# Who widens the counts: two of ten tiles move from GpSimd to VectorE, one from ScalarE to VectorE

## The chip, the cores and the metric

The kernel runs on one core of a Trainium2 chip. The time is the device time of one execution in microseconds (us). The core has a matrix engine (TensorE, PE), three engines for elementwise work (VectorE is DVE, ScalarE is ACT, GpSimd is POOL) and DMA queues. Every engine runs its own instructions strictly in program order and waits for the others on semaphores.

## The reference, cut to what matters

The model is a chain of four graph layers on 1250 nodes with 512 features and 20000 edges. The first two layers contain a mean over the neighbours of a node:

```
agg = jax.ops.segment_sum(x[src], dst, num_segments=n)          # layer 0
mean_agg = agg / jnp.maximum(cnt, 1.0)[:, None]
...
agg = jax.ops.segment_sum(msg, edge_index[1], num_segments=N)   # layer 1, msg = xn[edge_index[0]]
agg = agg / jnp.maximum(deg, 1.0)[:, None]
```

The kernel does each of these sums as a matrix product of the features with a matrix of edge counts.

## The kernel before, in words

The edge counts are built once, in the first 165 us, as an int16 matrix `cntT` of ten tiles: 125 source nodes on the partitions, 1250 destination nodes along the row. [...]

An aggregation (`aggregate` on TensorE) loops over four blocks `k` of 128 features, and in each over the ten tiles `j`. For one tile it issues six matmuls: two halves of the fp16-split features (`h_pair`) times three column pieces (512, 512, 226) of the widened tile. All ten tiles add up in one PSUM tensor `psW[k % 2]`. A group of three tiny matmuls closes the block and signals `agg_full`. VectorE then multiplies the block by the reciprocal degree into `aggT`, in one instruction in layer 0 and in a pair in layer 1, and signals `agg_taken` (and `agg_read`). Block k may start when block k-2 has been taken.

The widened tiles live in a ring of four buffers (`QUAD = 4`). Tile number n, counted over all blocks and both layers, may be written when TensorE has used tile n-4 (`cT_used` at n-3 or more). ScalarE writes tiles 0, 1, 2, 3, 4, 6, 7, 8 of each block (`BY_ACT`, through its helper `copy`, so the profile shows line 526). GpSimd writes tiles 5 and 9 (`BY_POOL`, line 464). TensorE waits for each tile by the count of whoever makes it (`widened`). A further branch for counts above 2048 (`big`) isn't taken.

Program order of VectorE around the two aggregations:

- Layer 0: `ln_stats(0)` ends with ten copies and splits of the normalised features (lines 897 and 900); the last split lets TensorE start. Then four instructions over 1250 columns prepare the reciprocal degree (lines 975 to 978). Then, per block, `counts_of_block` waits for `agg_full` and line 981 takes the block.
- Layer 1: behind the barrier `phase_end(dve, 3)` four pairs of additions correct `hT` (lines 1083 and 1084). Then, per block, the wait for `agg_full` and the pair of lines 1094 and 1096. Ahead of that wait, in blocks 1 and 2, stands `score_weights` (lines 1077 to 1080), ten instructions that prepare layer 2.

ScalarE and GpSimd have nothing but the widening to do during the blocks. Behind the four blocks TensorE goes on with the dense product of the layer.

Of the kernel before, what the change touches and what calls it, by code (L numbers as in the profile page):

```python
# [22 lines left out]
TILES, ROWS = 10, 125  # L23
KD = D // 128
# [22 lines left out]
QUAD = 4  # L47
# [27 lines left out]
def gnn_program(nc, a, out, layers=4):  # L75
    ctx = ExitStack()
    with ctx:
# [11 lines left out]
        cntT = sb("cntT", [128, TILES, N], I16)  # L89
# [63 lines left out]
        def region(off, shape, dt=F32):  # L153
# [47 lines left out]
        cntT_16 = [[region(o, [N], F16) for o in base] for base in (  # L201
            [G + 14750 + 625 * i for i in range(5)], [G + 14750, G + 15375, G + 5000, G + 5625, G + 6250])]
# [69 lines left out]

            return ps[:, 0:2 * PB * VA].rearrange("p (h b d) -> p h b d", h=2, b=PB)

        BY_ACT = (0, 1, 2, 3, 4, 6, 7, 8)
        BY_POOL = (5, 9)

        def widened(l, k, j):

            own, signal = (BY_POOL, "cP_wide") if j in BY_POOL else (BY_ACT, "cT_wide")  # L280
            return signal, len(own) * (l * KD + k) + own.index(j) + 1

        def acc_view(ps):
# [6 lines left out]
            edge_cols group_bounds bounds_turned bounds_set consts_set hot0_made hot1_made hot2_made hot3_made  # L290
            hot0_free hot1_free hot2_free hot3_free tile_counted counts_f32 mask_made bars_set counts_turning
            counts_turn_read deg_split deg_turned deg_row_out deg_wide ln_ready h_made h_turned hT_made
            x_plus_h h1_made h_split cT_wide cT_used cP_wide lo_wide lo_made lo_used agg_full agg_taken agg_read w_turned
            w_turn_read y_full y_out y_stats y_scaled y_started z_turned x_updated  qk_full qk_out v_full v_out
            proj_turned proj_out sq_made diag_full diag_out uk_full uk_max kmax_all kbias_set kf_exp
            kf_made uq_full uq_max qf_exp  qf_turned qfT_out kv_full kv_out at_full at_out at_turned
# [6 lines left out]
        S = {n: sem(n) for n in names}  # L303
# [18 lines left out]
        def after(eng, signal, count):  # L322

            if not isinstance(count, int) or count > 0:
                eng.wait_ge(S[signal], count)
# [128 lines left out]
        @block.gpsimd  # L454
        def _(pool):
            done = Order(pool, S["pool_done"])

            def widen(l):

                for k in range(KD):  # L460
                    for j in BY_POOL:
                        n = TILES * (l * KD + k) + j
                        pool.wait_ge(S["cT_used"], n - QUAD + 1)
                        pool.tensor_copy(cntT_16[l][n % QUAD][0:ROWS, :], cntT[0:ROWS, j, :]).then_inc(S["cP_wide"], 1)

            many = dict(allow_small_or_imprecise_dtypes=True, channel_multiplier=0)
            done(pool.memset(ident[:, :], 1.0))
            pool.affine_select(out=ident[:, :], in_=ident[:, :], compare_op=ALU.is_equal, fill=0.0, base=0,
                               pattern=[[-1, 128]], channel_multiplier=1).then_inc(S["ident_set"], 1)
            pool.memset(bar_c[:, :], BARRED).then_inc(S["bars_set"], 1)  # L470
            pool.iota(tile_lo, pattern=[[ROWS, TILES]], base=0, **many)
            pool.iota(up_row, pattern=[[1, GROUPS]], base=1, **many)
            done(pool.iota(down_row, pattern=[[-1, GROUPS]], base=GROUPS, **many))
            done(pool.memset(zero_bf[:, :], 0.0))
            pool.iota(iota_h[:, :], pattern=[[1, N]], base=0, **many).then_inc(S["consts_set"], 1)
            pool.memset(keps_c[:, :], KEPS)
            done(pool.memset(half_c[:, :], 0.0))
            for r in range(2):
                pool.memset(half_c[DH * r:DH * r + DH, r:r + 1], 0.5)
            done(pool.memset(sel[:, :, :], 0.0))  # L480
            for r in range(3):
                done(pool.affine_select(out=sel[:, :, :], in_=sel[:, :, :], compare_op=ALU.not_equal, fill=1.0, base=-r * TILES,
                                        pattern=[[-1, TILES], [0, 128]], channel_multiplier=1))
            pool.wait_ge(S["ident_set"], 1)
            pool.tensor_copy(ident_bf[:, :], ident[:, :]).then_inc(S["sel_set"], 1)
            pool.memset(hint_c[:, :], HINT)
            done(pool.memset(fold[:, :], 0.0))
            for r in range(2):
                done(pool.affine_select(out=fold[:, :], in_=fold[:, :], compare_op=ALU.not_equal, fill=1.0, base=-r * DH,
                                        pattern=[[-1, DH]], channel_multiplier=1))  # L490
            pool.memset(barred_c[:, :], -BARRED)
            done(pool.memset(ident_neg[:, :], 0.0))
            pool.affine_select(out=ident_neg[:, :], in_=ident_neg[:, :], compare_op=ALU.not_equal, fill=-1.0, base=0,
                               pattern=[[-1, 128]], channel_multiplier=1)
            done(pool.affine_select(out=sel_w[:, :], in_=ident_bf[:, :], compare_op=ALU.is_ge, fill=1.0, base=ROWS - 1,
                                    pattern=[[0, 128]], channel_multiplier=-1))

            phase_end(pool, 1)

            for t in range(TILES):  # L500
                pool.wait_ge(S["h_made"], t + 1)
                pool.tensor_tensor(x_nm[0:ROWS, t, :], x_nm[0:ROWS, t, :], h32[t % RING][0:ROWS, :], ALU.add).then_inc(S["x_plus_h"], 1)
            widen(0)
            phase_end(pool, 2)
            for i in range(2):
                half = slice(H // 2 * i, H // 2 * i + H // 2)
                pool.wait_ge(S["uk_max"], H // 2 * (i + 1))
                pool.partition_all_reduce(kmaxa[:, half], kmax[:, half], 128, RMAX).then_inc(S["kmax_all"], 1)
            phase_end(pool, 3)
            widen(1)  # L510
            phase_end(pool, 4)
            pool.wait_ge(S["hT_made"], 3 * TILES)
            pool.memset(v_gat[0:ROWS, :, :, DH], 1.0).then_inc(S["ones_set"], 1)
            pool.wait_ge(S["cols_out"], 1)
            for h in range(1, H):
                shift_of(pool, done, h)
            phase_end(pool, 5)
            pool.wait_ge(S["w_maxed"], 1)
            pool.partition_all_reduce(w_all[:, :], w_most[:, :], 128, RMAX).then_inc(S["w_spread"], 1)
            phase_end(pool, 6)  # L520
# [3 lines left out]
        def _(act):  # L524
# [77 lines left out]
            def widen(l, big):  # L602

                for k in range(KD):
                    for j in BY_ACT:
                        n = TILES * (l * KD + k) + j
# [196 lines left out]
        def _(dve):  # L803
# [82 lines left out]
            def ln_stats(l):  # L886
# [8 lines left out]
                for t in range(TILES):  # L895
                    dve.wait_ge(S["h_turned"], TILES * l + t + 1)
                    dve.tensor_copy((hT if l < 3 else hT3)[:, :, t * ROWS:(t + 1) * ROWS], psS[t % 2][:, 0:KD * ROWS].rearrange("p (k c) -> p k c", k=KD)).then_inc(S["hT_made"], 1)
                    if l < 2:
                        dve.wait_ge(S["h1_made"], TILES * l + t + 1)
                        stt(h_pair[1][0:ROWS, t, :], h32[t % RING][0:ROWS, :], HS, h_pair[0][0:ROWS, t, :], ALU.mult, ALU.subtract).then_inc(S["h_split"], 1)  # L900

            def counts_of_block(l, k, big):

                with dve.If(big > 0):
                    for j in range(TILES):
                        dve.wait_ge(S["lo_wide"], TILES * (l * KD + k) + j + 1)
                        tt(cntT_16[l][QUAD][0:ROWS, :], cntT[0:ROWS, j, :], cntT_16[l][QUAD][0:ROWS, :], ALU.subtract).then_inc(S["lo_made"], 1)
                dve.wait_ge(S["agg_full"], l * KD + k + 1)
# [63 lines left out]

            big = has_big_count(dve)
            ln_stats(0)
            done(ts(rdeg_b, pos_b, 1.0, None, ALU.max))
            done(dve.reciprocal(rdeg_b, rdeg_b))
            done(ts(rdeg_b, rdeg_b, 1.0 / HS, None, ALU.mult))
            done(ts(pos_b, pos_b, 1.0, None, ALU.min))
            for k in range(KD):
                counts_of_block(0, k, big)  # L980
                tt(aggT[:, k, :], psW[k % 2][:, 0:N], rdeg_b, ALU.mult).then_inc(S["agg_taken"], 1)
            dve.wait_ge(S["vec_in"], 16 * 10)
# [3 lines left out]
            if layers >= 2:  # L986
# [86 lines left out]
                def score_weights(r):  # L1073
# [5 lines left out]
                    done(tt(prod, wb_row, half, ALU.mult))  # L1079
                    return dve.tensor_reduce(c16[:, own], prod, AX, ALU.add)  # L1080

                for f in range(KD):
                    tt(hT[:, f, 0:NPERF], hT[:, f, 0:NPERF], oT[:, f, :], ALU.add)
                    done(ts(hT[:, f, NPERF:N], hT[:, f, NPERF:N], oT[:, f, NPERF - 1:NPERF], None, ALU.add))
                for k in range(KD):
                    if k == 1:
                        dve.wait_ge(S["w_gat_in"], 16 * KD)
                        dve.wait_ge(S["gat_w_in"], 48)
                        done(score_weights(0))
                        done(tt(c16[:, 0:H], c16[:, 0:H], ab_row, ALU.add))  # L1090
                    if k == 2:
                        score_weights(1).then_inc(S["wa_made"], 1)
                    counts_of_block(1, k, big)
                    stt(aggT[:, k, :], psW[k % 2][:, 0:N], scl1[:, k:k + 1], rdeg_b, ALU.mult, ALU.mult).then_inc(S["agg_taken"], 1)
                    dve.wait_ge(S["agg_taken"], KD + k + 1)
                    stt(aggT[:, k, :], pos_b, shf1[:, k:k + 1], aggT[:, k, :], ALU.mult, ALU.add).then_inc(S["agg_read"], 1)
# [656 lines left out]
```

## Time and profile before

| | us |
|---|---|
| median of 3 runs | 1310.76 |
| lowest, highest | 1310.09, 1312.12 |
| the profiled execution, whole | 1311.84 |
| its span, first to last instruction | 1310.1 |

In the profile, a group line names line, engine, operation and tiles, then the count, the busy time and the mean of one in ns, and the idle time before it with what ended it. A timeline row is start, length, engine, line, operation, count of merged instructions and, in brackets, the idle time ahead of it and who ended it. A windows row gives the busy time of each engine in a stretch with the number of instructions, then the clock that TensorE was granted (1.00 is 2.4 GHz, 0.50 is 1.2 GHz) and the DMA share. A waits row is the waiting line, what it waited for, the sum in us, how many times, and the longest.

### The profile page before, as it was taken

Reading aid. Unit: us, or ns where it says so; the run is one execution under the profiler, and the core shown is the slowest. Engines: PE = TensorE matmul, PEld = TensorE weight load, DVE = VectorE, ACT = ScalarE, POOL = GpSimd, SP = SyncE. Lnnn points to the kernel's source line nnn. Section 1 sums busy time; section 2 is a strip of 40 time slices with the busy share of each in tenths; the row PEclk is TensorE's granted clock in tenths of the full one; section 3 lists DMA queues with packets and bytes.
Section 4 is the critical chain, followed back from the end, with each engine's and each line's share of the span. In section 5 each row is a group of like instructions: output and inputs, shape, how many; then the busy total and the mean of one; then the engine's idle time right before and its main releaser. Section 6 shows DMA issues by size and latency. Waiting matters only on the chain.

```text
span 1310.1 us, 16906 instructions
## 1 busy us (share of the span) xinstructions
PE 1178.8 (90%) x5857; PEld 736.3 (56%) x5857; DVE 924.0 (71%) x1663; ACT 708.2 (54%) x885; POOL 65.2 (5%) x115
## 2 busy tenths in 40 slices
PE   4999959997998986979999999859988999999996
PEld 3666635554785544435444544434545777777775
DVE  6999873105455697778998896673116888888885
ACT  1232368202556667148778777531115777777774
POOL 3000042000001100000000000000000000000000
PEclk8999959997899996979999999979997999999999
DMA  4000000003003000201111100020011111110102
GB/s 148 5 1 1 1 1 2 1 1 129 1 1 89 2 1 1 81 23 42 42 42 42 42 23 3 1 96 1 1 24 25 25 26 25 26 25 1 26 1 79
DMA packets 24769, 36.15 MB, mean 28 GB/s; under 512 B 11874, under 2 KB 13204, under 8 KB 24694
## 3 DMA queue, kind: packets, MB, share of 16 engines
q1 hardware_dynamic: 24694, 35.14, 9.0%
q8 instruction: 49, 0.80, 0.3%
q14 instruction: 26, 0.21, 0.1%
HBM read 26.03 MB, written 2.70 MB: 22 GB/s over the span
## 4 chain that ended last, share of the span: by engine, by line
PE 56%; DVE 11%; ACT 5%; issue 3%; DMA 0%; SPq 0%; ACTq 0%; DVEq 0%; POOLq 0%
PE wide L58 15%; PE wide L1613 12%; PE wide L1243 7%; PE small L1697 5%; PE wide L1601 3%; PE wide L1603 3%; PE small L1655 2%; ACT arena L797 2%; PE small L1243 2%; DVE arena L1126 2%; PE wide L1402 1%; PE small L1710 1%; DVE arena L1150 1%; DVE bn L812 1%; DVE bns L915 1%
## 5 line engine op out<-in xcount | busy, mean ns | idle before, releaser
L58 PE MATMUL wide<-arena 125*125 (+7 forms) x2028 | 487.2, 389 | 33.3 <-DVE arena L873 12.6
L58 PEld LDWEIGHTS wide<-arena 125*125 (+4 forms) x2028 | 270.6, 141 | 226.7 <-issue 144.1
L1613 PE MATMUL wide<-arena 125*65 125x512 f32 (+1 forms) x480 | 181.5, 514 | 0.0
L1243 PE MATMUL small<-ident,arena 125*128 125x125 f32 (+5 forms) x438 | 85.8, 347 | 62.1 <-ACT arena L593 32.0
L1150 DVE TENSOR_TENSOR arena<-wide,arena 125x1250 f32<-125x1250 f32 x80 | 116.7, 1459 | 35.2 <-PE wide L1603 35.2
L725 ACT ACTIVATE arena<-arena,b 125x1250 f32<-125x1250 f32 x80 | 106.7, 1336 | 58.4 <-PE wide L1613 54.0
L782 ACT ACTIVATE arena<-wide 125x1000 f16<-125x1000 f32 x80 | 80.8, 1010 | 80.8 <-PE wide L1243 80.8
L1243 PE MATMUL wide<-ident,arena 125*125 125x125 f32 (+2 forms) x874 | 116.8, 282 | 6.5 <-ACT arena L797 3.5
L797 ACT ACTIVATE arena<-arena,neg_max,unit 125x1250 f32<-125x1250 f32 x80 | 114.3, 1429 | 10.5 <-DVE neg_max L1231 10.5
L1613 PEld LDWEIGHTS wide<-arena 125*65 125x65 f32 x480 | 63.1, 138 | 101.0 <-issue 94.5
L1204 DVE SCALAR_TENSOR_TENSOR arena<-wide,arena 125x1000 f16<-125x1000 f32 x80 | 95.9, 1198 | 33.8 <-ACT arena L782 33.8
L1126 DVE CUSTOM_DVE_ANT_0 arena<-arena,cnt 125x1250 bf16<-125x1250 f32 x80 | 116.1, 1451 | 1.5 <-DVE b_max L1126 1.5
L1697 PE MATMUL small<-arena 125*128 125x250 f16 x800 | 112.7, 271 | 1.4 <-DVE arena L1206 1.4
L1243 PEld LDWEIGHTS small<-ident,arena 125*128 125x128 f32 (+5 forms) x438 | 69.2, 218 | 78.9 <-issue 37.0
L1243 PEld LDWEIGHTS wide<-ident,arena 125*125 125x125 f32 (+2 forms) x874 | 104.6, 188 | 14.8 <-ACT arena L797 8.0
L872 DVE TENSOR_SCALAR arena<-arena 125x1250 f16 x196 | 106.1, 541 | 7.2 <-issue 5.5
L754 ACT ACTIVATE arena<-arena,b 125x1250 f32<-125x1250 f32 x80 | 105.8, 1324 | 5.8 <-DVE arena L1150 5.8
L526 ACT ACTIVATE arena<-wide 65x512 f32<-65x512 f32 (+4 forms) x50 | 29.7, 641 | 133.5 <-PE wide L1305 110.3
L1697 PEld LDWEIGHTS small<-arena 125*128 125x128 f16 x800 | 72.1, 98 | 27.8 <-issue 20.2
L526 ACT ACTIVATE arena<-cntT 125x1250 f16<-125x1250 int16 x64 | 74.5, 1233 | 14.3 <-PE wide L58 14.1
L1601 PE MATMUL wide<-arena,sel_w 128*125 128x512 bf16 (+1 forms) x240 | 58.2, 351 | 12.5 <-DVE arena L1150 9.1
L1228 DVE CUSTOM_DVE_ANT_0 arena<-wide,cnt 125x1250 f32<-125x1250 f32 x40 | 58.0, 1451 | 10.8 <-PE wide L58 10.8
(241 smaller groups left out, 1221.0 us busy)
## 6 DMA issues: line engine op xcount, KB each, us to landing
arena<-rows_kept SPq DMA_DIRECT2D x16, 625.0 KB, 5.6
arena<-arena SPq DMA_DIRECT2D x40, 156.2 KB, 2.8
arena<-in_L_gnn_W SPq DMA_DIRECT2D x3, 1024.0 KB, 7.6
x_nm<-in_x SPq DMA_DIRECT2D x2, 1250.0 KB
out<-x_nm SPq DMA_DIRECT2D x1, 2187.5 KB
arena<-in_L_gnn_W_l SPq DMA_DIRECT2D x1, 1024.0 KB, 5.8
arena<-in_L_gnn_W_r SPq DMA_DIRECT2D x1, 1024.0 KB, 8.1
arena<-in_L_gnn_Wk SPq DMA_DIRECT2D x1, 1024.0 KB, 5.5
```

Source lines behind the costliest of these rows:

```text
L58: mm = pe.matmul(ps[0:rows, lo:hi], lhsT, rhs[:, lo:hi], start=start, stop=stop, skip_group_check=True)
L526: return act.activation(dst, src, ACT.Copy, **k)
L725: act.activation(ring[n % RINGS][0:ROWS, :], t_bc[h % 2][0:ROWS, :], ACT.Relu, scale=0.8, bias=b08[0:ROWS, h, t:t + 1]).then_inc(S["relu2_ ...
L754: act.activation(row, row, ACT.Exp, bias=b02[0:ROWS, h, t:t + 1]).then_inc(S["exp2_made"], 1)
L797: act.activation(row, row, ACT.Exp, bias=neg_max[0:ROWS, n % TILES:n % TILES + 1], scale=unit[0:ROWS, 0:1], accum_out=den3[0:ROWS, n:n + 1 ...
L872: ts(hot_src[0:ROWS, n % 2, g, :], iota_h[0:ROWS, :], e_col[0:ROWS, 1, k, g:g + 1], None, ALU.is_equal)
L1126: dve.tensor_tensor_reduce(junk[0:ROWS, :], b_bc[h % 2][0:ROWS, :], mask[0:ROWS, i, :], 1.0, 2 * NEG, ALU.subtract, ALU.max, b_max[0:ROWS, ...
L1150: tt(row, psW[0][0:ROWS, 0:N], row, ALU.add).then_inc(S["z2_made"], 1)
L1243: return pe.transpose(dst, src, ident[0:k, 0:k])
L1601: pe.matmul(psW[0][0:ROWS, lo:hi], sel_w[:, 0:ROWS], ln_hi[:, t, lo:hi], start=True, stop=False)
L1613: m = pe.matmul(psW[1][0:VA, lo:hi], v_gat[0:ROWS, t, h, :], ring[n % RINGS][0:ROWS, lo:hi], start=(t == 0), stop=(t == TILES - 1))
L1697: m = pe.matmul(small[:, 0:2 * ROWS], v_pair[0:ROWS, j, h, :, :].rearrange("p c d -> p (c d)"), turned[pair % 2][0:ROWS, j, 2 * part:2 * p ...
```

## The change

Tiles 3, 6 and 9 of each block are widened by VectorE, the other seven by ScalarE, none by GpSimd. The rule of the ring and the order in which TensorE uses the tiles stay. VectorE's three casts of a block are put into its program as one group, with the waits on `cT_used` between them: block 0 of layer 0 behind `ln_stats(0)` and ahead of line 975; block 0 of layer 1 ahead of lines 1083 and 1084; every later block at the head of its turn of the loop, so ahead of `score_weights` in layer 1 and behind the instructions that take the previous block.

```diff
-        BY_ACT = (0, 1, 2, 3, 4, 6, 7, 8)
-        BY_POOL = (5, 9)
+        BY_ACT = (0, 1, 2, 4, 5, 7, 8)
+        BY_DVE = (3, 6, 9)
...
-            own, signal = (BY_POOL, "cP_wide") if j in BY_POOL else (BY_ACT, "cT_wide")
+            own, signal = (BY_DVE, "cV_wide") if j in BY_DVE else (BY_ACT, "cT_wide")
...
@@ GpSimd: the helper and both calls, widen(0) and widen(1), go
-                        pool.wait_ge(S["cT_used"], n - QUAD + 1)
-                        pool.tensor_copy(cntT_16[l][n % QUAD][0:ROWS, :], cntT[0:ROWS, j, :]).then_inc(S["cP_wide"], 1)
...
@@ VectorE
+            def widen(l, k):
+                for j in BY_DVE:
+                    n = TILES * (l * KD + k) + j
+                    after(dve, "cT_used", n - QUAD + 1)
+                    dve.tensor_copy(cntT_16[l][n % QUAD][0:ROWS, :], cntT[0:ROWS, j, :]).then_inc(S["cV_wide"], 1)
...
             ln_stats(0)
+            widen(0, 0)
             done(ts(rdeg_b, pos_b, 1.0, None, ALU.max))
             done(dve.reciprocal(rdeg_b, rdeg_b))
             done(ts(rdeg_b, rdeg_b, 1.0 / HS, None, ALU.mult))
             done(ts(pos_b, pos_b, 1.0, None, ALU.min))
             for k in range(KD):
+                if k >= 1:
+                    widen(0, k)
                 counts_of_block(0, k, big)
...
+                widen(1, 0)
                 for f in range(KD):
                     tt(hT[:, f, 0:NPERF], hT[:, f, 0:NPERF], oT[:, f, :], ALU.add)
                     done(ts(hT[:, f, NPERF:N], hT[:, f, NPERF:N], oT[:, f, NPERF - 1:NPERF], None, ALU.add))
                 for k in range(KD):
+                    if k >= 1:
+                        widen(1, k)
                     if k == 1:
                         dve.wait_ge(S["w_gat_in"], 16 * KD)
```

## Rows read from the trace of the kernel before

**Rows 1.** The page: busy time of the engines; then the chain that ended last.

```profile
PE 1178.8 (90%) x5857; PEld 736.3 (56%) x5857; DVE 924.0 (71%) x1663; ACT 708.2 (54%) x885; POOL 65.2 (5%) x115
...
PE 56%; DVE 11%; ACT 5%; issue 3%; DMA 0%; SPq 0%; ACTq 0%; DVEq 0%; POOLq 0%
```

**Rows 2.** Windows over one inner block of layer 0 and of layer 1.

```profile
206.84:217.60 10.76, 10.76 (x63) 5.77 (x60) 1.46 (x1) 9.15 (x9) 2.46 (x2) 1.00 0.01 2
418.53:429.30 10.77, 10.77 (x63) 5.77 (x61) 10.35 (x11) 9.16 (x9) 3.12 (x2) 1.00 0.01 2
```

**Rows 3.** Waits: PE and ACT in 193.5 to 240, PE in 405.5 to 452.

```profile
PE wide L58 <- DVE arena L900: 2.4, 1, 2.4
...
ACT arena L526 <- PE wide L58: 8.6, 8, 2.2
...
PE wide L58 <- ACT arena L526: 3.3, 1, 3.3
```

**Rows 4.** Timeline of layer 0 around its first block.

```profile
193.46 0.80 DVE L975 TENSOR_SCALAR arena<-arena 128x1250 f32<-128x1250 f32 x1
...
193.59 13.16 PE L58 MATMUL wide<-arena 125*128 125x512 f16 x60 [2.44 <-DVE arena L900]
...
194.29 7.97 DVE L976 RECIPROCAL arena<-arena 128x1250 f32<-128x1250 f32 x1
...
202.55 1.63 POOL L464 CAST arena<-cntT 125x1250 f16<-125x1250 int16 x1 [3.32 <-PE wide L58]
203.13 1.72 DVE L978 TENSOR_SCALAR arena<-arena 128x1250 f32<-128x1250 f32 x1
...
206.84 10.84 PE L58 MATMUL wide<-arena 125*128 125x512 f16 x60
206.95 1.46 DVE L981 TENSOR_TENSOR arena<-wide,arena 128x1250 f32<-128x1250 f32 x1 [2.10 <-PE wide L1340]
```

**Rows 5.** Timeline of layer 1 across its first three blocks.

```profile
404.48 0.43 DVE L1083 TENSOR_TENSOR arena<-arena 128x256 f32<-128x256 f32 x1 [0.35 <-ACTq L319]
...
408.14 0.73 DVE L1084 TENSOR_SCALAR arena<-arena 128x994 f32<-128x994 f32 x1
...
414.25 1.22 POOL L464 CAST arena<-cntT 125x1250 f16<-125x1250 int16 x1 [3.19 <-PE wide L58]
...
418.64 1.52 DVE L1094 SCALAR_TENSOR_TENSOR arena<-wide,scl,arena 128x1250 f32<-128x1250 f32 x1 [9.76 <-PE wide L1340]
420.19 1.52 DVE L1096 SCALAR_TENSOR_TENSOR arena<-arena,shf 128x1250 f32<-128x1250 f32 x1
...
421.63 1.71 DVE L1077 TENSOR_TENSOR arena<-arena 128x512 f32<-128x512 f32 x1
...
431.01 1.52 DVE L1094 SCALAR_TENSOR_TENSOR arena<-wide,scl,arena 128x1250 f32<-128x1250 f32 x1 [0.25 <-DVE c L1090]
...
434.29 0.68 DVE L1077 TENSOR_TENSOR arena<-arena 128x512 f32<-128x512 f32 x1
...
441.57 1.51 DVE L1094 SCALAR_TENSOR_TENSOR arena<-wide,scl,arena 128x1250 f32<-128x1250 f32 x1
```

**Rows 6.** Groups of VectorE by line and shape: nearest operations to the new cast.

```profile
L872 DVE TENSOR_SCALAR arena<-arena 125x1250 f16 x196 | 106.1, 541 | 7.2 <-issue 5.5 <-PE wide L58 1.6
...
L931 DVE TENSOR_TENSOR arena<-arena 125x1250 bf16<-125x1250 f32 x10 | 14.5, 1453 | 6.9 <-ACT arena L620 6.7
```

**Rows 7.** Windows around idle stretches of PE, for the granted clock.

```profile
402.63:405.97 3.34, 0.00 (x1) 0.03 (x2) 2.55 (x12) 2.69 (x7) 0.00 (x0) 1.00 0.07 9
...
406.60:410.00 3.40, 3.40 (x12) 1.43 (x10) 2.21 (x5) 3.40 (x4) 0.16 (x1) 0.50 1.06 338
...
826.50:828.60 2.10, 0.30 (x3) 0.06 (x2) 2.10 (x3) 1.41 (x2) 0.00 (x0) 1.00 0.00 0
...
878.50:880.90 2.40, 0.00 (x1) 0.00 (x0) 2.10 (x10) 1.26 (x2) 0.00 (x0) 1.00 0.00 0
...
881.10:884.30 3.20, 3.20 (x4) 1.17 (x4) 1.97 (x3) 0.00 (x0) 0.00 (x0) 0.50 0.00 0
```

More of the change, by code:

```diff
@@ L292, in gnn_program @@
             counts_turn_read deg_split deg_turned deg_row_out deg_wide ln_ready h_made h_turned hT_made
-            x_plus_h h1_made h_split cT_wide cT_used cP_wide lo_wide lo_made lo_used agg_full agg_taken agg_read w_turned
+            x_plus_h h1_made h_split cT_wide cT_used cV_wide lo_wide lo_made lo_used agg_full agg_taken agg_read w_turned
             w_turn_read y_full y_out y_stats y_scaled y_started z_turned x_updated  qk_full qk_out v_full v_out
@@ L456, in _ @@
             done = Order(pool, S["pool_done"])
[L458 to L462, printed above, removed]
-                        pool.wait_ge(S["cT_used"], n - QUAD + 1)
-                        pool.tensor_copy(cntT_16[l][n % QUAD][0:ROWS, :], cntT[0:ROWS, j, :]).then_inc(S["cP_wide"], 1)
             many = dict(allow_small_or_imprecise_dtypes=True, channel_multiplier=0)
@@ L502, in _ @@
                 pool.tensor_tensor(x_nm[0:ROWS, t, :], x_nm[0:ROWS, t, :], h32[t % RING][0:ROWS, :], ALU.add).then_inc(S["x_plus_h"], 1)
-            widen(0)
             phase_end(pool, 2)
@@ L509, in _ @@
             phase_end(pool, 3)
-            widen(1)
             phase_end(pool, 4)
```

## Prediction

> **What bounds the kernel now.** I read the page first: TensorE is busy 90% of the span, and on the chain that ended last it holds 56% against 11% for VectorE and 5% for ScalarE [rows 1]. That is an average over six stages, and the change touches two of them, so I took the windows over single blocks next. An inner block has TensorE busy from end to end at clock 1.00 in both layers (10.76 of 10.76 us, 10.77 of 10.77 us) [rows 2]. The waits say the same from the other side: through the four blocks of layer 0 TensorE waited once, at their start, 2.4 us for VectorE's last split, and through those of layer 1 once, 3.3 us for the first widened tile. ScalarE, on the contrary, waited eight times for TensorE to free a buffer [rows 3]. So the supply of widened tiles is never late today. Its makers run ahead until the ring of four is full. A block takes 10.84 us for 60 matmuls, 1.084 us a tile, and 10.92 us from start to start with the closing group (206.84 + 10.92 = 217.76) [rows 4]. No part of the change touches this, so it has nothing to gain there. The question is only whether VectorE delivers tiles 3, 6 and 9 in time. A tile 3 is wanted 3.25 us after its block starts.
>
> VectorE is idle through most of a block of layer 0 (1.46 us busy), but not in layer 1 (10.35 us busy in the second block) [rows 2]. And an in-order engine is late by what stands ahead of an instruction, not by its busy share.
>
> **The cost of one cast.** The trace shows no int16 to fp16 copy on VectorE. Below, the nearest row is a one-input operation on 125x1250 of 2-byte data, 0.541 us; above, the slow rate of an operation of this length, 1.453 us [rows 6]. I take 0.54, the row nearest in size, width of data and number of inputs, and keep 1.45 for the range. Going from one instruction to the next costs VectorE 0.03 us (193.46 + 0.80 to 194.29) [rows 4]. The first matmul starts 0.05 us behind the end of what it waited for (the split ahead of 193.59 ended at 193.54).
>
> A rule to weigh here: the Trainium skill, "VectorE: DVE Perf Modes", section "The perf-mode tier table", gives a copy of 2-byte data in SBUF four elements a cycle and 693 ns for 2048 of them. By its breakdown (some 158 fixed cycles and 1250/4 at 0.96 GHz) the cast would take an estimated 0.49 us, and the sum below would be 0.4 us less. No run here shows whether the conversion from int16 keeps that rate; without it the upper bound applies.
>
> **Layer 0.** Tiles 0 to 2 come from ScalarE as before, tile 3 from VectorE right behind the split, well ahead of need. Then VectorE stands at tile 9, which may be written once tile 5 has been used. GpSimd's cast of tile 9 waited for the same event and began at 202.55 [rows 4]. Behind this wait now stand lines 975 to 978, which began at 193.46 before. From the start of line 975 to that of line 978 is 9.67 us, nearly all of it the 7.97 us reciprocal [rows 4]. Line 978 costs a further 0.80 like line 975; its 1.72 in the trace includes a delay beside a GpSimd cast. So:
>
> 202.55 + 0.54 + 0.03 (tile 9) = 203.12; + 9.67 + 0.84 = 213.63; line 981 takes block 0, + 1.46 + 0.03 = 215.12; tile 3 of block 1, + 0.54 + 0.05 = 215.7.
>
> TensorE wants that tile at 206.84 + 3.25 = 210.1. **Stall 5.6 us** in block 1. In blocks 2 and 3 VectorE has only line 981 ahead of tile 3: 0.11 + 1.49 + 0.54 = 2.1 us after the block's end against some 3.4, hidden, and hidden also with a cast of 1.45. ScalarE's casts are ready sooner in the stall and cost nothing.
>
> **Layer 1, block 0 to 1.** `widen(1, 0)` goes ahead of the corrections of `hT`, and waits for tile 5 of block 0: GpSimd began on the same event at 414.25 [rows 5]. The corrections took 404.48 to 408.87 (408.14 + 0.73), 4.39 us [rows 5]. 414.25 + 0.57 + 4.42 = 419.24. `agg_full` is there by then; the pair of lines 1094 and 1096 takes 3.07 us (418.64 to 421.71), so 422.34; tile 3, + 0.54 + 0.05 = 422.9. It is wanted at 418.53 + 3.25 = 421.8. **Stall 1.1 us.**
>
> **Block 1 to 2.** From now on VectorE's round from one tile 9 to the next tile 3 sets the pace. It starts when tile 5 has been used: 0.15 to notice, 0.57 for tile 9, `score_weights(0)`, the pair 3.10, tile 3 with 0.59. From line 1077 at 421.63 to line 1094 at 431.01 is 9.38 us, of which the first instruction took 1.71 where its twin took 0.68 [rows 5], and a third one was longer by 0.71 beside the next GpSimd cast. Without casts there it is 7.6. Sum 12.0 us. TensorE itself needs, from tile 5 used to tile 3 wanted, four tiles, the closing group and three tiles: 4.34 + 0.15 + 3.25 = 7.74. **Stall 4.3 us.**
>
> **Block 2 to 3.** The same with `score_weights(1)`, 434.29 to 441.57, 7.28 us [rows 5]: 0.15 + 0.57 + 7.28 + 3.10 + 0.59 = 11.7 against 7.74. **Stall 3.9 us.** Behind block 3 everything follows as before, later by the sum.
>
> Here a rule counts on the change's side. The clearest row is line 1077, 1.71 us where its twin took 0.68 [rows 5]. The Trainium skill, "GPSIMD Engine Reference", section "Specifications", has GpSimd's SBUF interfaces shared with VectorE, with contention for instructions with two SBUF inputs, and line 1077 is one; the trace agrees. The sum above already uses undisturbed durations; with the disturbed ones it would be about 2.6 us higher.
>
> **The clock.** After 2.40 us of idleness ending at 880.90 TensorE ran at 0.50 in 881.10 to 884.30, and after 3.34 us ending at 405.97 at 0.50 in 406.60 to 410.00; after the 1.80 us within 826.50 to 828.60 it stayed at 1.00 [rows 7]. The stalls of 5.6, 4.3 and 3.9 us lie with the former, that of 1.1 with the latter. A fall costs half the time spent at 0.50: 3.40 us make 1.7. At the upper end is the first block of layer 0, which began slow and took 13.16 us against 10.84, 2.3 more [rows 4]. I take 2.0 three times, **6.0 us**. The slow tiles come right behind the stall, before tile 5, so VectorE's next round doesn't hide them.
>
> **Sum.** 5.6 + 1.1 + 4.3 + 3.9 = 14.9, and 6.0 for the clock: 20.9 us more. GpSimd's sixteen casts and ScalarE's eight end off the path and give nothing back. The profiled execution took 1311.84 us in all for a span of 1310.1, which makes 1332.7; it was 1.1 above the median of the runs, so the predicted median is 1310.76 + 20.9 = **1331.7**.
>
> **The rivals.**
> - *The stalls come, the clock holds.* It speaks for it that each stall is short against the stage and dense matmuls stand around it; against it, the fall after 2.40 us. 14.9 more: 1325.7.
> - *The cast runs at the slow rate.* Each of the four late rounds holds two casts, so 8 x 0.91 = 7.3 us on top: 20.9 + 7.3 = 28.2, 1339.0. The conversion of the type speaks for it, the 0.541 us row against it.
> - *Not slower: the tile supply paces TensorE.* The six matmuls of a tile have 2500 columns, 1.042 us at 2.4 GHz, and take 1.084. If the gap were waiting for ScalarE's signals, seven casts instead of eight would close part of it: up to 8 x 0.4 = 3.2 us less, 1307.6. It decides only where VectorE's round stays below TensorE's 7.74 us; reckoned, it is 12.0. ScalarE's eight waits for TensorE speak against it [rows 3].
> - *Deeper loss.* Falls of the clock last longer, or catch the 1.1 us stall as well: 3 to 5 us more, 1335 to 1337.
>
> **How the numbers follow.** Forecast 0.66, its own range 1327 to 1336; clock holds 0.12; slow cast 0.09; deeper loss 0.08; not slower 0.05. The range 1324 to 1340 takes in both bounds of the cast and both of the clock. A measurement tells about 0.2% (2.6 us) from no change. Of the last case 0.02 is faster and 0.02 the same, and 0.01 is a small loss; all others are slower: 0.96.
>
> **What would show it.** In the waits, TensorE's matmuls of line 58 wait for VectorE's cast four times, 5.6, 1.1, 4.3 and 3.9 us, each at tile 3 of a block; none in blocks 2 and 3 of layer 0. Line 975 starts near 203 instead of 193.5. The group of the cast shows 24 instructions of 0.54 us. The windows behind the three long stalls show 0.50 for 3 to 5 us. Line 1077 shows no 1.71. The prediction is wrong if TensorE is busy through blocks 1 as before, if the wait falls on another tile or engine, or if the loss is outside the two aggregations.

## The result and the profile after

| | before, us | changed, us |
|---|---|---|
| median | 1311.44 (4 runs) | 1333.07 (4 runs) |
| lowest, highest | 1310.09, 1312.67 | 1330.12, 1333.29 |
| span of the profiled execution | 1310.1 | 1331.5 |

The ratio is 1.016, 95% interval 1.0142 to 1.0178: 21.6 us slower, where 20.9 had been forecast. The title counts the change net; tile by tile, 9 goes from GpSimd to VectorE, 3 and 6 from ScalarE to VectorE, and 5 from GpSimd to ScalarE.

First the waits of the changed kernel, TensorE only, for the stretch from 193.5 to 250 and then for 405 to 480 (waiting line, what it waited for, sum in us, times, longest). Line 897 is VectorE's new cast, which widens one tile from int16 to fp16.

```profile
PE wide L58 <- DVE arena L897: 5.4, 1, 5.4
PE wide L58 <- DVE arena L890: 2.4, 1, 2.4
...
PE wide L58 <- DVE arena L897: 8.2, 3, 3.9
PE wide L58 <- ACT arena L516: 3.3, 1, 3.3
```

The 2.4 and the 3.3 us are the old waits of [rows 3]. New are four waits for VectorE, 13.6 us together. The timeline shows what VectorE did while TensorE stood still. Layer 0:

```profile
203.50 0.49 DVE L897 CAST arena<-cntT 125x1250 f16<-125x1250 int16 x1 [2.71 <-PE wide L58]
203.90 0.81 DVE L973 TENSOR_SCALAR arena<-arena 128x1250 f32<-128x1250 f32 x1
...
204.74 7.97 DVE L974 RECIPROCAL arena<-arena 128x1250 f32<-128x1250 f32 x1
...
207.81 3.37 PE L58 MATMUL wide<-arena 125*128 125x512 f16 x18
...
214.67 1.46 DVE L981 TENSOR_TENSOR arena<-wide,arena 128x1250 f32<-128x1250 f32 x1 [0.28 <-DVE arena L976]
216.05 0.88 DVE L897 CAST arena<-cntT 125x1250 f16<-125x1250 int16 x2
216.59 9.20 PE L58 MATMUL wide<-arena 125*128 125x512 f16 x42 [5.41 <-DVE arena L897]
```

TensorE does 18 matmuls, three tiles, and stops at 211.18. VectorE had taken up its next work at 203.90 (line 975 in [rows 4], there at 193.46), and the cast of tile 3 comes only at 216.05. Layer 1, blocks 1 to 3:

```profile
430.42 7.64 PE L58 MATMUL wide<-arena 125*128 125x512 f16 x42 [0.93 <-DVE arena L897]
...
433.83 0.49 DVE L897 CAST arena<-cntT 125x1250 f16<-125x1250 int16 x1 [3.07 <-PE wide L58]
434.24 0.68 DVE L1077 TENSOR_TENSOR arena<-arena 128x512 f32<-128x512 f32 x1
...
438.14 3.37 PE L58 MATMUL wide<-arena 125*128 125x512 f16 x18
...
444.88 0.88 DVE L897 CAST arena<-cntT 125x1250 f16<-125x1250 int16 x2
445.41 9.12 PE L58 MATMUL wide<-arena 125*128 125x512 f16 x42 [3.90 <-DVE arena L897]
...
461.34 9.30 PE L58 MATMUL wide<-arena 125*128 125x512 f16 x42 [3.35 <-DVE arena L897]
```

Line 1077 now takes 0.68 where [rows 5] had 1.71. Behind the stall of 0.93 the last 42 matmuls of a block take 7.64 us, all at full clock; behind the long ones they take 9.20, 9.12 and 9.30. The windows (last figures: granted clock, DMA share, GB/s) show why:

```profile
216.59:219.80 3.21, 3.21 (x10) 1.43 (x11) 0.34 (x1) 0.91 (x1) 0.00 (x0) 0.50 0.00 0
445.41:448.50 3.09, 3.09 (x9) 1.33 (x10) 0.34 (x1) 0.78 (x1) 0.00 (x0) 0.50 0.00 0
462.20:465.60 3.40, 3.40 (x12) 1.36 (x11) 0.00 (x0) 1.85 (x2) 0.00 (x0) 0.51 0.00 0
```

From the first aggregation matmul to the first of the dense product, layer 0 took 53.11 us (194.60 to 247.71) against 46.01 before, and layer 1 57.17 (413.56 to 470.73) against 45.32: 7.1 and 11.9, together 19.0 of the 21.4 us between the spans. The other 2.4 lie outside and are spread: 1.0 ahead of layer 0, 0.5 less between the layers, 2.0 behind layer 1. The new cast, a group of 24:

```profile
L897 DVE CAST arena<-cntT 125x1250 f16<-125x1250 int16 x24 | 11.3, 485 | 42.5 <-PE wide L58 42.1 <-ACTq L319 0.3
```

### The profile page after: what moved, and what is told of

The parts are those of the page before. It is cut to its first block, busy times and chain, and to the rows that moved or that the text cites. A ratio compares the mean times of both kernels' runs of the same rounds, so it can differ in the third digit from the quotient of the medians.

```text
span 1331.5 us, 16906 instructions
## 1 busy us (share of the span) xinstructions
PE 1179.6 (89%) x5857; PEld 733.0 (55%) x5857; DVE 930.7 (70%) x1687; ACT 700.5 (53%) x877; POOL 44.3 (3%) x99
## 4 chain that ended last, share of the span: by engine, by line
PE 54%; DVE 13%; ACT 5%; issue 3%; DMA 0%; SPq 0%; ACTq 0%; DVEq 0%; POOLq 0%
PE wide L58 13%; PE wide L1616 12%; PE wide L1246 7%; PE small L1700 5%; PE wide L1604 3%; PE wide L1606 3%; PE small L1658 2%; PE small L1246 2%; ACT arena L787 2%; DVE arena L1129 2%; PE wide L1405 1%; PE small L1713 1%; DVE arena L1153 1%; DVE bn L802 1%; DVE bns L912 1%
## 5 line engine op out<-in xcount | busy, mean ns | idle before, releaser
L58 PE MATMUL wide<-arena 125*125 (+7 forms) x2028 | 492.5, 392 | 46.9 <-DVE arena L897 13.6
L1246 PE MATMUL small<-ident,arena 125*128 125x125 f32 (+5 forms) x438 | 80.7, 332 | 68.7 <-ACT arena L583 32.5
L1246 PEld LDWEIGHTS small<-ident,arena 125*128 125x128 f32 (+5 forms) x438 | 64.8, 204 | 84.8 <-issue 37.0
L516 ACT ACTIVATE arena<-cntT 125x1250 f16<-125x1250 int16 x56 | 66.6, 1237 | 40.5 <-PE wide L58 40.4
```

Of the source, the lines that this page charges most:

```text
L58: mm = pe.matmul(ps[0:rows, lo:hi], lhsT, rhs[:, lo:hi], start=start, stop=stop, skip_group_check=True)
L516: return act.activation(dst, src, ACT.Copy, **k)
L1246: return pe.transpose(dst, src, ident[0:k, 0:k])
```

## The experiments

Theory A: VectorE's casts cost nothing themselves; four come late because of what its program has ahead of them, TensorE stops, and its clock falls. Rivals: VectorE's casts slow TensorE wherever they run (B); the loss is outside the aggregations (C); the clock falls for another reason. "Before" is the kernel before, run again beside each experiment; its median moved between 1311.15 and 1312.83.

**One layer at a time.** Each kernel has a table of makers, one letter a tile: A for ScalarE, V for VectorE, P for GpSimd.

```diff
-        BY_ACT = (0, 1, 2, 4, 5, 7, 8)
-        BY_DVE = (3, 6, 9)
+        MAKERS = [['AAAVAAVAAV'] * KD, ['AAAAAPAAAP'] * KD]   # e1: layer 0 changed
+        MAKERS = [['AAAAAPAAAP'] * KD, ['AAAVAAVAAV'] * KD]   # e2: layer 1 changed
```

> Layer 0 as in the changed kernel (VectorE makes tiles 3, 6, 9), layer 1 as before (ScalarE eight, GpSimd two). Theory A, VectorE comes late by what stands ahead of its cast: one stall, 5.4 us at tile 3 of block 1 of layer 0, and one fall of the clock, 1.7; so 7.1 us above before, 1318.5. Rival B, VectorE casts slow TensorE down wherever they run (each tile a little, spread over all blocks): about half of the 21.6, that is 10 to 11 us, with blocks 2 and 3 longer than 10.92. Rival C, the loss sits outside the aggregations: another split than 7 to 12.

> Layer 0 as before, layer 1 as in the changed kernel. Theory A: stalls of 0.9, 3.9 and 3.4 us at tile 3 of blocks 1, 2 and 3 and two falls of the clock, 3.5 us; 11.8 us above before, 1323.2. Rival B: 10 to 11 us spread over the tiles. Rival C: the sum of this run and the one for layer 0 misses the 21.6 of the whole change.

Measured: e1 1319.58 against 1311.15 before, ratio 1.0062 (1.0045 to 1.0079), 8.4 us. Its waits show one stall on the cast, the second row being the old one:

```profile
PE wide L58 <- DVE arena L912: 5.4, 1, 5.4
PE wide L58 <- DVE arena L905: 2.4, 1, 2.4
```

e2 1326.65, ratio 1.0114 (1.0098 to 1.0131), 15.5 us, with stalls of 0.93, 3.91 and 3.36. The stalls are as theory A has them. Rival B's even split over the layers isn't there, and blocks 2 and 3 of e1's layer 0, with VectorE's casts in them, still take 10.92 us from start to start (226.09, 237.01). As for rival C, outside the two aggregations the profiled execution of e1 lost 0.5 of 8.2 us and that of e2 2.1 of 16.1: a part, not the bulk. But 15.5 is above the 11.8 expected, 8.4 is above the 7.1, and 8.4 + 15.5 is 2.3 more than the whole change costs, which is within the intervals. The windows of e2 show where its profiled execution lost more: behind the same two stalls the slow stretch lasts twice as long, and the last 42 matmuls take 10.59 and 10.42 us.

```profile
437.30:444.00 6.70, 6.04 (x18) 2.55 (x19) 0.99 (x3) 2.49 (x2) 0.00 (x0) 0.50 0.00 0
454.00:461.20 7.20, 5.84 (x17) 2.53 (x18) 1.70 (x3) 2.49 (x2) 0.00 (x0) 0.53 0.00 0
```

**Place or chance?** The same kernel as e2, and the changed kernel, each profiled again; and e2 with some VectorE work of no use between the layers.

> The kernel of e2_layer1 once more, for a second profile. There two stalls of 3.9 and 3.4 us were followed by 6.8 us at 0.50 each, where the changed kernel had 3.4 us behind stalls of the same length. If the length of a slow stretch is fixed by the place in the program: 6.8 us again, blocks 2 and 3 with 10.6 and 10.4 us for their last 42 matmuls. If it hangs on chance in each execution: one or both at 3.4 us, with 9.1 to 9.3.

> The changed kernel once more, for a second profile. Fixed by place: the three slow stretches last 3.4 us again and blocks 1, 2 and 3 take 9.2, 9.1 and 9.3 us for their last 42 matmuls, total 1333. By chance: one or more at 6.8 us, another total within 3 us. The stalls themselves stay at 5.4, 0.9, 3.9 and up to 3.4 us in either case.

Measured: e10 1327.05, with stalls of 0.93, 3.91 and 3.36, and now 9.08 and 9.30 us for the last 42 matmuls, the short stretches. e11 1331.09, with stalls of 5.41, 0.93, 3.91 and 3.36; here the last 42 matmuls took 10.55 in block 1 of layer 0, 10.25 in block 2 of layer 1 and 7.64, without any slow stretch, in block 3, and block 0 of layer 1, slow before and after, ran at 1.00 (10.88). Two of these, from e11's timeline:

```profile
215.25 10.55 PE L58 MATMUL wide<-arena 125*128 125x512 f16 x42 [5.41 <-DVE arena L897]
...
461.62 7.64 PE L58 MATMUL wide<-arena 125*128 125x512 f16 x42 [3.36 <-DVE arena L897]
```

So each stall is fixed to 0.1 us by the program, and what the clock does behind it is not: in one kernel it costs 0, 1.5 to 1.7 or 2.6 to 2.9 us a stall. Yet e10 came out near the total of e2 with shorter stretches in layer 1. Between the two profiled executions (spans of 1325.3 and 1326.2) its layer 1 aggregation is 2.6 us shorter, and the four other stretches are each 0.3 to 0.7 longer, 1.7 together.

```diff
             add_back(0, True)
+            junk_in = head_sum[0:ROWS, :, :, :].rearrange("p u t d -> p (u t d)")
+            done(dve.memset(junk_in, 1.0))
+            done(dve.reciprocal(junk_in[:, 0:160], junk_in[:, 0:160]))
             phase_end(dve, 2)
```

> The kernel of e2_layer1 with some 1.8 us of VectorE work of no use ahead of the barrier between layer 0 and layer 1 (a memset of 640 columns and a reciprocal of 160), so that all of layer 1 starts later against the program's start. If the slow stretches depend only on the stalls: 1.8 above e2_layer1, 1328.5. If they depend on when in time a stall falls: away from that by up to 3.4 either way, and the stretches behind the stalls change between 3.4 and 6.8 us.

Measured: 1326.54 (4 runs), ratio 1.0108 (1.009 to 1.0126), the same as e2 within the intervals. The experiment is inconclusive. The added work ran (0.59 and 1.15 us), but from the end of layer 0's aggregation to the start of layer 1's it was 166.2 us, as before (166.4), so layer 1 was not moved. It is a third profile of e2's stalls (0.93, 3.90, 3.36), with short stretches behind the long two (9.13 and 9.30).

**The clock alone.** TensorE gets work of no use to fill the stalls.

```diff
                         signal, count = widened(l, k, j)
+                        for _ in range({(0, 1): 24, (1, 2): 17, (1, 3): 15}.get((l, k), 0) if j == 3 else 0):
+                            pe.matmul(psS[0], h_pair[0][0:ROWS, 0, 0:128], h_pair[0][0:ROWS, 0, :], start=True, stop=True)
                         pe.wait_ge(S[signal], count)
```

> The changed kernel, with dense matmuls of no use put ahead of TensorE's wait in the three long stalls (24, 17 and 15 of 512 columns, into a PSUM bank that nobody reads then). They fill the idle time and add nothing to the results. If the idle time is what lowers the clock: the clock stays at 1.00 through blocks 1 to 3 and the 1.7, 1.7 and 1.8 us come back; block 3 then waits up to 0.5 longer, since the slow tiles hid a part of VectorE's round; 4.7 us less than the changed kernel, 1328.4. If the falls have another cause: the same as the changed kernel, 1333, with 0.50 in the same windows.

Measured: 1326.19, ratio 1.0117 (1.01 to 1.0134), 15.0 us above before, where the changed kernel had 21.6. The stretch with the filled stall, and the two behind filled stalls:

```profile
211.20:216.57 5.37, 5.14 (x25) 2.16 (x23) 5.02 (x6) 0.25 (x1) 0.00 (x0) 1.00 0.00 0
216.57:224.14 7.57, 7.57 (x42) 4.01 (x43) 0.83 (x2) 5.48 (x5) 0.00 (x0) 1.00 0.01 2
...
440.33:447.90 7.57, 7.57 (x43) 4.02 (x43) 4.33 (x8) 5.48 (x5) 0.00 (x0) 1.00 0.01 2
```

VectorE is as late as before (TensorE goes on at 216.57, as at 216.59), but the clock stays at 1.00, and the 42 matmuls take 7.64, 7.63 and 7.64. Chance is a poor rival: of the 13 unfilled stalls of 3.3 us or more in six profiles (changed, e1, e2, e9, e10, e11) 12 have a fall, begun in the stall or within 0.9 us behind it; of the three filled ones none. So idleness in the stall brings the fall. Block 3 was expected to wait up to 0.5 longer and did not: TensorE goes on 6.72 us after the block's start in both kernels. The gain, 6.6 us with both kernels taken against their own before, is more than the 4.7 expected, by less than the intervals allow. In the profiles the spans differ by 9.6, e4's being its fastest execution (1323.66). The blocks behind the stalls account for 4.7 of it (1.56, 1.49 and 1.66), block 0 of layer 1, at 1.00 here as in e11, for 1.6, and the rest lies outside the aggregations; what in it is chance isn't shown.

**The same split, in time.** VectorE makes the same 24 tiles, each where it is due.

```diff
             done(ts(rdeg_b, pos_b, 1.0, None, ALU.max))
-            done(dve.reciprocal(rdeg_b, rdeg_b))
+            done(dve.reciprocal(rdeg_b[:, 0:N // 2], rdeg_b[:, 0:N // 2]))
+            widen(0, 1, (3,))
+            done(dve.reciprocal(rdeg_b[:, N // 2:N], rdeg_b[:, N // 2:N]))
+            widen(0, 1, (6,))
...
+            widen(0, 1, (9,))
...
-                widen(1, 0)
+                widen(1, 0, (3,))
                 for f in range(KD):
...
+                widen(1, 0, (6, 9))
                 for k in range(KD):
                     if k >= 1:
-                        widen(1, k)
+                        widen(1, k, (6,))
+                    if k == 3:
+                        widen(1, k, (9,))
...
-                        done(score_weights(0))
+                        done(score_weights(0, lambda: widen(1, 1, (9,))))    # called half way
...
                     counts_of_block(1, k, big)
+                    if k < KD - 1:
+                        widen(1, k + 1, (3,))
```

> The same split of the ten tiles as in the changed kernel, but VectorE's program has each cast where it is due: in layer 0 the reciprocal is cut into two halves of 625 columns with the cast of tile 3 of block 1 between them, in layer 1 tile 3 of the next block goes ahead of the pair that takes the block, tile 9 into the middle of the score weights, and the corrections of hT go ahead of tiles 6 and 9. Theory A: no stall over 0.5 us, time as before within 0.2%, 1309 to 1314. Rival B (the casts themselves slow TensorE or their own engine too much): 5 to 20 us above before. If ScalarE's eighth tile paced TensorE: 3 us below before.

Measured: 1311.84 against 1311.15, ratio 1.0005 (0.9996 to 1.0015). The timeline of VectorE where the changed kernel had its first stall:

```profile
202.84 4.06 DVE L989 RECIPROCAL arena<-arena 128x625 f32<-128x625 f32 x1
206.93 0.49 DVE L912 CAST arena<-cntT 125x1250 f16<-125x1250 int16 x1
207.34 4.05 DVE L991 RECIPROCAL arena<-arena 128x625 f32<-128x625 f32 x1
```

The cut reciprocal costs 0.1 us more than the whole one, and the cast between its halves is early. Through both aggregations TensorE's waits at line 58 have the two old rows and no other. This decides between A and B: 24 casts on VectorE, in time, cost 0.7 us with an interval from 0.5 less to 2.0 more, against 21.6 for the same casts late.

**ScalarE's eighth tile.** MAKERS is 'AAAPAAPAAP' throughout.

> ScalarE seven tiles, as in the changed kernel, but tiles 3, 6 and 9 made by GpSimd, which has nothing else to do in the blocks (1.23 us a cast). If the supply by ScalarE paced TensorE, relieving it of a tile would give up to 0.4 us a block, 3 us in all: 1308. Theory A (TensorE is never waiting for tiles before, and only VectorE's other work makes them late): same as before, 1311, within 1.5; blocks 10.92 us from start to start.

Measured: 1311.71 against 1312.01, ratio 1.0 (0.9991 to 1.0009); a block of layer 0 still takes 10.92 us from start to start (205.88 to 216.80). ScalarE did not pace TensorE.

**A better version?** VectorE's short cast helps where TensorE waits for the very first tile of layer 1, and the filler may help ahead of both aggregations.

```diff
+        MAKERS[1][0] = 'VAAAAPAAAP'          # e6; all other blocks 'AAAAAPAAAP'
...
                 project(3)
+                idle_work(7)                  # e7: seven matmuls of 512 columns, three behind the barrier
                 phase_end(pe, 3)
+                idle_work(3)
...
                     m.then_inc(S["h_turned"], 1)
+                    if l == 0 and t >= 2:     # e8: also between the transposes of layer 0
+                        if t == 2:
+                            pe.wait_ge(S["h_split"], 1)
+                        idle_work(1 if t < TILES - 1 else 5, psW[1], 384 if t < TILES - 1 else D)
```

> The kernel before, with one tile given to VectorE: tile 0 of block 0 of layer 1, cast in 0.49 us where ScalarE takes 1.23, right behind the barrier, with nothing ahead of it. TensorE waits for this tile, 3.3 us. Theory A, place decides: the wait shortens by 0.7 to 0.9 us, and the clock may or may not fall behind it; 1310.3, and 1308.6 if it doesn't fall. If something else ends the wait as late: no change.

> As e6_first, and ten matmuls of no use in TensorE's idle time ahead of layer 1's aggregation, seven ahead of the barrier and three behind it. If idle time lowers the clock, block 0 of layer 1 runs at 1.00 and takes 10.84 instead of 12.48: 1.6 less than e6_first, 2.5 less than before, 1308.6. If the fall behind this wait has another cause: as e6_first. They could also delay the first tile by up to 0.2.

> As e7_first_warm, and matmuls of no use between the transposes ahead of layer 0's aggregation too, one of 384 columns behind each tile's transposes from the third on and five of 512 at the end, where TensorE runs at 0.50 with gaps of 0.4 us and then waits 2.4 us. If filling the gaps brings the clock up before the first block: block 0 takes 10.84 instead of 13.16, another 2.3 less, 1306.3. If TensorE stays at 0.50: as e7_first_warm, or up to 0.5 slower, where a filler is in the way of a transpose.

Measured: e6 1311.57, ratio 0.9995 (0.9986 to 1.0004); e7 1311.42, 0.9997 (0.9988 to 1.0006); e8 1309.02, 0.9976 (0.9967 to 0.9985), all against 1312.01. In e6 the wait fell from 3.34 to 2.49, the clock fell all the same (block 0 12.48). In e7 block 0 ran at 1.00 and took 10.81, so the local effects came as expected, but of the 2.5 us expected below before the total shows 0.6: a miss. In e7's profile the part behind layer 1 was 860.9 us long against 858.8 before, with a slow stretch in layer 2's start that lasted longer (17.1 us at 0.50 against 13.7). The longer one is also in the profiles of the changed kernel, e2, e8, e9 and e10, the shorter one in e1, e3, e4, e5, e6 and in e11, which is the changed kernel again. So one kernel can have either; that it is chance in e7 isn't shown. e8 misses its 1306.3 by e7's miss, while its step from e7, 2.4 us, is the 2.3 expected. In e8 the clock rose during the transposes, fell once more, and was up for the first block. Before ([rows 4], the first block of 13.16 us) and in e8:

```profile
182.00:193.59 11.59, 6.55 (x25) 4.25 (x25) 11.59 (x17) 11.20 (x16) 9.80 (x7) 0.50 0.00 0
```

```profile
182.00:189.00 7.00, 3.90 (x25) 2.36 (x23) 7.00 (x11) 6.60 (x11) 7.00 (x5) 0.98 0.00 0
189.00:193.00 4.00, 3.68 (x14) 2.22 (x14) 4.00 (x7) 4.00 (x6) 3.42 (x3) 0.57 0.00 0
194.22:204.97 10.75, 10.75 (x60) 5.76 (x60) 10.25 (x4) 8.58 (x8) 2.46 (x2) 1.00 0.01 2
```

The first block takes 10.82. e8 is the fastest kernel of the study, 3.0 us below before, and what makes it so is work of no use on TensorE, not the new split.

## Why the prediction was right

- *No gain to be had.* Right. Before the change TensorE waited for a widened tile only ahead of layer 1's first block, and taking a tile from ScalarE gave nothing (e5).
- *The cast at 0.54 us.* 0.485 measured. The Trainium skill's page "VectorE: DVE Perf Modes", section "The perf-mode tier table", weighed there, gave an estimate of 0.49: the measurement agrees, and the conversion from int16 keeps the rate.
- *Layer 0, 5.6 us.* 5.41, at tile 3 of block 1, with no stall in blocks 2 and 3. Counted as the prediction counts, from 3.25 us behind the block's start, it is 5.5, and those of layer 1 are 1.0, 4.0 and 3.5.
- *Layer 1, 1.1, 4.3 and 3.9 us.* 0.93, 3.90 and 3.35. VectorE's rounds were a little shorter than reckoned. From its start on tile 9 to TensorE's restart they took 11.58 us (433.83 to 445.41) and 11.03 (450.31 to 461.34), where the terms without the notice make 11.86 and 11.54. The two casts gave 0.2 us a round and the pair 0.1, the score weights 0.2 in the second round and nothing in the first; the durations of overlapping rows had been added end to end. The low clock behind the second stall was over by 448.5, before tile 5 had been used (450.2), so it hid nothing of the next round, as forecast.
- *The undisturbed durations.* Right for line 1077, which took 0.68. The 7.28 taken for `score_weights(1)` still held a delay beside a GpSimd cast; without those casts it took 7.11 (450.71 to 457.82). The two-input contention that the Trainium skill gives in "GPSIMD Engine Reference", section "Specifications", went with them, in agreement.
- *The clock, three falls of 2.0 us.* Three falls came, none behind the 0.93 us stall. By the last 42 matmuls against 7.64 they cost 1.6, 1.5 and 1.7 us in the profiled execution, 4.7 together instead of 6.0. As a fixed price the term was wrong in kind: e11, the same kernel, had 2.9, 2.6 and 0. That it is a cost of idleness is shown by e4.
- *The total.* Counted the prediction's way, the stalls made 14.1 of 14.9 and the clock 4.7 of 6.0; the two aggregations together lost 19.0 of the 20.9 forecast. That the total came so near is luck: 2.4 us came from outside them, which no term had. They lie within what single executions differ by (1330.1 to 1333.3). But the part behind layer 1 took 860.1 to 860.8 us in all five profiles with long unfilled stalls in layer 1 (changed, e2, e9, e10, e11) and 858.8 to 859.6 in before, e1, e3, e4, e5 and e6, while e7 and e8, also without such stalls, had 860.9. Whether a part of it is systematic stays open.
- *Place, not price.* That the loss comes from the order of VectorE's program and not from giving it the casts was argued from the timeline, and e3 shows it: the same 24 casts, 0.7 us from before (0.5 less to 2.0 more).

## What to carry to other kernels

Before a small operation is given to an engine that looks idle, write down for each of its deadlines what the engine's program has ahead of it, waits included: a group of three casts with a wait inside ties all the later work to that wait. If one long instruction stands in the way, cut it and put the short one in between; 0.1 us bought back 5.4 here. And a stall of a few us on TensorE costs more than its length, by an amount that differs between executions of one kernel, so compare medians and count a range for it.

## What the runs showed of the hardware

- A copy of 125x1250 from int16 to fp16 takes 0.485 us on VectorE, 1.23 on ScalarE, and 1.23 on GpSimd where VectorE isn't in its way (1.63 and 1.89 beside it).
- In or just behind stalls of 3.4 to 5.4 us TensorE's clock went to 0.50 for 3.4 or 6.8 us, or once not at all, in the same kernel (changed and e11). It also fell behind a wait of 2.49 us (e6). Behind 0.93 us it never did, in six profiles.
- Matmuls whose result nobody reads held the clock at 1.00 through a stall (e4) and raised it in a stretch of sparse transposes that had been at 0.50 (e8).
- A reciprocal of 1250 fp32 columns on VectorE takes 7.97 us, ten times a multiplication; two halves take 4.06 and 4.05.
